# A recommendation tower on one core: a ring of two blocks of gathers in place of three, and transposes moved in the program of TensorE

## The reference, cut to what matters

```python
e = stack([tbl_f[ids[:, f]] for f in range(26)], axis=1)      # 512 x 26 x 128
sd = einsum('bfd,bd->bf', e, dense)                            # each embedding with the dense row
ss = einsum('bfd,bgd->bfg', e, e)                              # all pairs of embeddings
z = concatenate([dense, sd, ss[:, iu, ju]], axis=1)            # upper triangle: 325 pairs
h = concatenate([z, dense], axis=1)                            # 607 columns
h = maximum(h @ W_top1 + b_top1, 0)                            # 512
h = maximum(h @ W_top2 + b_top2, 0)                            # 256
y = h @ W_top3                                                 # 1
```

## Time and profile before

| what | value |
|---|---|
| median of 3 runs | 132.18 us (131.85 to 134.35) |
| the profiled execution | 132.72 us |
| its span in the trace | 130.9 us |
| PE busy | 94.0 us (72%) |
| DVE busy | 73.7 us (56%) |
| POOL busy | 67.5 us (52%) |
| ACT busy | 61.8 us (47%) |
| granted clock of TensorE, mean | 0.896 |

### The profile page before, as it was taken

The page is one execution under the profiler, slowest core; times in us unless marked ns, Lnnn a source line. Parts: engine busy times, 40 slices in busy tenths (PEclk is TensorE's granted clock), DMA queues, the critical chain, the costliest instruction groups (busy, mean ns, idle before and its releaser), DMA issues.

```text
span 130.9 us, 3331 instructions
## 1 busy us (share of the span) xinstructions
PE 94.0 (72%) x1420; PEld 78.2 (60%) x1420; DVE 73.7 (56%) x170; ACT 61.8 (47%) x131; POOL 67.5 (52%) x70
## 2 busy tenths in 40 slices
PE   0089899999969999000547459397784997897892
PEld 0157688888858887000436349286674796786780
DVE  1387999999997835000008927264370731974621
ACT  3435591966908506300308909164370904964410
POOL 2878888787888787770831725538172560000000
PEclk9999999999999999965557756999999559999999
DMA  2999965947996121220110110102011110000000
GB/s 53 242 379 367 272 242 185 267 115 179 381 372 207 44 60 40 63 59 21 44 41 8 45 40 25 49 16 60 25 38 43 25 40 25 0 5 0 8 0 1
DMA packets 6849, 13.37 MB, mean 102 GB/s; under 512 B 2353, under 2 KB 3506, under 8 KB 6834
## 3 DMA queue, kind: packets, MB, share of 16 engines
q1 hardware_dynamic: 4112, 8.95, 21.4%
q0 software_dynamic: 2048, 4.20, 11.2%
q10 hardware_dynamic: 674, 0.01, 0.3%
HBM read 13.15 MB, written 0.00 MB: 100 GB/s over the span
## 4 chain that ended last, share of the span: by engine, by line
PE 44%; POOL 17%; issue 15%; DMA 7%; another core or an unknown queue 6%; ACT 6%; DVE 2%; DVEq 0%; ACTq 0%
POOL rows L294 17%; PE gram L371 12%; PE hidden L398 8%; PE second L415 6%; PE gram L342 6%; DMA rows<-in_tables_gather,idx 5%; PE stage L325 5%; PE hidden L387 3%; PE hidden L342 2%; ACT Z L492 2%; ACT ET L470 2%; ACT ET L482 2%; PE second L413 2%; DVE Z L568 2%
## 5 line engine op out<-in xcount | busy, mean ns | idle before, releaser
L294 POOL DMA_INDIRECT rows<-in_tables_gather,idx x64 | 66.8, 1044 | 39.0 <-issue 17.4
L568 DVE COPY Z<-gram 32x112 f32<-32x112 f32 (+3 forms) x72 | 23.0, 320 | 35.5 <-PE gram L371 34.6
L371 PE MATMUL gram<-ET 128*32 128x27 f32 x1024 | 17.0, 207 | 25.8 <-issue 12.8
L492 ACT COPY Z<-gram 32x112 f32<-32x112 f32 (+1 forms) x72 | 23.2, 322 | 23.7 <-PE gram L371 22.9
L371 PEld LDWEIGHTS gram<-ET 128*32 128x32 f32 x1024 | 14.1, 123 | 29.4 <-issue 26.0
L552 DVE TENSOR_SCALAR onehot<-ids,rowid 128x1024 fp32r<-128x1024 int16 (+1 forms) x48 | 28.7, 659 | 5.1 <-DMA ids<-in_ids_one 2.1
L342 PE MATMUL gram<-onehot,part 128*128 128x512 f32 x80 | 22.5, 434 | 6.6 <-DVE part L558 6.2
L342 PEld LDWEIGHTS gram<-onehot,part 128*128 128x128 f32 x80 | 16.4, 211 | 10.7 <-DVE onehot L552 6.2
L342 PE MATMUL hidden<-onehot,part 128*128 128x512 f32 x80 | 19.7, 397 | 0.6 <-issue 0.6
L342 PEld LDWEIGHTS hidden<-onehot,part 128*128 128x128 f32 x80 | 14.6, 188 | 3.7 <-issue 0.8
L558 DVE TENSOR_TENSOR part<-raw,part 128x1024 fp32r<-128x1024 f32 (+2 forms) x11 | 12.1, 1123 | 3.1 <-issue 2.4
(11 more groups left out here) (38 smaller groups left out, 42.2 us busy)
## 6 DMA issues: line engine op xcount, KB each, us to landing
raw<-in_tables_one SPq DMA_DIRECT2D x9, 512.0 KB
ids<-in_ids_one SPq DMA_DIRECT2D x4, 256.0 KB, 5.5
rows<-in_tables_gather,idx POOLq DMA_INDIRECT x64
W1s<-in_W_pairs SPq DMA_DIRECT2D x1, 768.0 KB
W1d<-in_W_dense SPq DMA_DIRECT2D x1, 512.0 KB
W2s<-in_W_top SPq DMA_DIRECT2D x1, 512.0 KB
raw<-in_tables_one SPq DMA_DIRECT2D x1, 384.0 KB
ids<-in_ids_one SPq DMA_DIRECT2D x2, 128.0 KB, 3.6
```

The source lines that it names most:

```text
L294: pool.indirect_dma_start(out=rows[:, m % ROWS_RING, :], out_offset=None, in_=x["tables_gather"], in_offset=bass.IndirectOffsetOnAxis(ap=i ...
L371: last = pe.matmul(gram[p % 2][32 * i:32 * i + 32, NV * j:NV * (j + 1)], ET[:, VP * b:VP * (b + 1)], ETv[:, b, 0:NV], start=True, stop=True)
L492: last = act.copy(dst, src)
L568: last = dve.tensor_copy(dst, src)
```

## The change

The ring holds two blocks (8 gathers) where it held three (12). By L292 and L293, the gathers of block n now wait for the transposes of block n-2, not n-3, and block 2 is the first that waits, not block 3. The transposes of b4, b5 and b6 stand later among the look-ups: b4 after chunk 1 of group 4, b5 after its chunk 4, b6 after chunk 1 of group 5. The transposes of b8 to b12 stand one piece earlier, after pieces 0 to 4, and those of b13 stand after the Gram products of piece 5, ahead of its layers, where they stood behind the layers.

```diff
-ROWS_RING = 3 * GB
+ROWS_RING = 2 * GB
...
         AMID = {(0, 7): ["dense"], (1, 3): ["b0"], (2, 1): ["b1"], (2, 5): ["b2"], (3, 1): ["b3"],
-                (3, 6): ["b4"], (4, 3): ["b5"], (4, 7): ["b6"], (5, 7): ["b7"]}
-
-        SOON = {1: ["b8"], 2: ["b9"], 3: ["b10"], 4: ["b11"], 5: ["b12"]}
-        LATER = {5: ["b13"], 6: ["b14"], 7: ["b15"]}
+                (4, 1): ["b4"], (4, 4): ["b5"], (5, 1): ["b6"], (5, 7): ["b7"]}
+
+        SOON = {p: [f"b{p + 8}"] for p in range(6)}
+        LATER = {6: ["b14"], 7: ["b15"]}
```

## The result

The changed kernel takes 141.97 us (median of 4 runs, 141.34 to 142.56) beside 132.30 us for the kernel before: a ratio of 1.074 (95% interval 1.066 to 1.083). In a later comparison it was 1.077 (1.070 to 1.084). The prediction had the sign and the mechanism, but 137.4 us with a range up to 141.0; it was 4.6 us short. (Some executions of any of these kernels are slower at a lower granted clock; all ratios leave them out, and of e2 only one of four executions was free of this, so it has no ratio.) The profiled execution took 141.38 us, with a span of 139.5 us.

The account below looks back on a forecast made before the run. The prediction took a loop to bound the kernel: POOL's gathers stop PE, whose transposes release POOL. 132.72 + 0.75 (look-ups) + 4.50 (Gram stage) = 137.97, less 0.54, gave 137.4 us; range 132.0 to 141.0.

Parts of the forecast that it names:

- The loop: Gram stage: transposes release POOL, its four gathers stop PE, PE then finishes the piece and makes the next transposes; 7.69 us each.
- Six rounds: Gram stage: pieces 1 to 6 run beside the gathers of blocks 10 to 15; 46.14 us at 7.69 each.
- the five pairs of before: Earlier trace, blocks 10 to 14: PE comes free 0.97 to 1.04 us after each block's last gather.
- the look-up term: Look-ups: block 9's gathers end at 67.6, against 66.85 for block 10 before; +0.75 us (-3.65 to +1.85).
- products cost 0.235 us each: Look-ups: PE's price per product, from 16 products at 47.98 to 51.74, used for the 24 products of group 3.
- the end of the stop: Piece 0: PE is free 0.99 us after block 9's last gather; with the piece's rest, 2.09 us to b8's transposes.
- the late signal: End of the look-ups before: PE's signal reached ACT and POOL only after POOL's run of gathers; POOL restarted 3.00 us later.
- Gathers of block 3 in time: Rival, look-ups: block 3's gathers miss the weight loads and land in time, POOL stays at the low end; 133.0 us, chance 0.20.
- PE's stops not due to gathers: Rival: the stops are PE's own, say in its supply of small instructions, and signals come promptly; 127.6 us, chance 0.10.
- Late signals in the look-ups: Rival: chunks of groups 4 and 5 are signalled late while POOL runs, so b5 and b6 release it late; 140.4 us, chance 0.20.

Follow-up runs that it names:

- e2: Kernel before with the changed order of transposes but its ring of three blocks; 136.1 us against 133.0, from the one comparable execution.
- e11: Kernel before with blocks 10 to 15 loaded by SP as plain rows, not gathered by POOL (wrong rows); 117.0 us, ratio 0.866.
- e16: Kernel before with blocks 10 to 15 loaded by SP as plain rows, plus five POOL memsets at each of their releases; 116.2 us, ratio 0.867.
- e5: Kernel before with a ring of four blocks, on the chip where PE does not creep; 109.41 us against 109.35, ratio 1.010.
- e14: Changed kernel with SP loading the weights and masks only after b3's transposes; 139.0 us against 134.1 for the kernel before, ratio 1.038.
- e12: Kernel before, ring of three, with only the gathers of blocks 10 to 15 waiting for block n-2; 133.7 us against 132.7, ratio 1.008.
- e17: Kernel before with b13 to b15 ahead of the layers of pieces 5 to 7, blocks 10 to 14 waiting for block n-2; 133.3 us, ratio 0.998.
- e18: Kernel before with only b13, b14 and b15 moved ahead of the layers of pieces 5, 6 and 7, more rounds; 131.86 us against 132.96, ratio 0.991.
- e1: Kernel before with only the ring cut to two blocks, old order of transposes; 141.6 us against 133.0, ratio 1.059.
- e3: Changed kernel with b4, b5 and b6 back at their old places among the look-ups; 142.2 us, ratio 1.070 to the kernel before.
- e10: The changed kernel measured again, on a chip where PE creeps; 143.4 us against 132.7 for the kernel before.
- e4: Kernel before with only b13, b14 and b15 moved ahead of the layers of pieces 5, 6 and 7; first measurement, ratio 0.989.
- e15: Kernel before with a ring of four blocks, on a chip where PE creeps; 138.3 us against 134.1, ratio 1.034.

## Why the prediction was short

**The loop was right.** Six rounds were in the trace, each with PE free 0.85 to 0.94 us after the block's last gather (78.73 and 79.65 for block 10, 117.37 and 118.31 for block 15). From b8 to the end of piece 6 they took 46.57 us, where 46.14 had been forecast: 0.43 of the difference. e11 and e16 show that the cause is the right one, which the five pairs of before had only made likely. The rules cited from the Trainium skill (SBUF — State Buffer, Who interferes with whom), that a DMA never contends with a compute engine and that PE waits on nobody, don't hold for indirect transfers where PE creeps: the earlier trace rows and the 0.866 of e11 go against them. SP's plain loads in e11, and the gathers on e5's chip, agree with them.

**The step that failed is the look-up term**, "67.6 - 66.85 = +0.75 us". The path was right, its sizes weren't: it measured 69.14 - 66.85 = +2.29. Block 2's first gather took 3.05 us beside DVE's L558, not 1.97, so block 3's last one started at 31.12, not 30.2. It took 7.06 us to land, as taken from the earlier trace rows, so PE waited 6.03 us for it, not 5.0. Then "products cost 0.235 us each", a size read at full clock, failed: the transposes of b3 took 1.09 us, not 0.6, and the 24 products behind them 7.10 us, not 5.6. Three windows of the changed kernel show why; the first is of all engines, the other two of PE alone (busy us and count, granted clock, DMA share, GB/s):

```profile
30.00:40.00 10.00, 3.97 (x17) 3.13 (x16) 7.58 (x11) 5.26 (x7) 7.19 (x7) 0.76 0.96 310
```

```profile
41.00:42.00 1.00, 1.00 (x4) 0.50 0.28 66
42.00:43.00 1.00, 1.00 (x5) 0.99 0.25 61
```

After PE had been idle for 6.03 us its granted clock was 0.50 up to 42 us, and then 1.00. In the kernel before, PE was idle for no more than 1.03 us here, and the clock was 1.00 from 30 to 50 us; in e14, with a wait of 2.44 us, it stayed at 1.00 too. DVE was held up meanwhile, but the one-hots of those 24 products had been made by 33.98, before the wait was over, so it had no part in this. The wait was paid for again: some 3 us of products at half clock are 1.5 us lost, and the transposes lost 0.5. All this put the end of b4's transposes at 48.41, not 46.0, and block 6 started at 48.68, not 46.3.

The gathers of block 6 took 0.7 us more than taken. On the other side, b7's signal was not late: ACT took b7 at 61.51, and block 9 followed block 8 after 0.30 us, where a pause of 1.9 us had been forecast. Those 1.6 us hid part of the error above: +2.4, +0.7 and -1.6 make the 1.5 us by which the term was short. That they partly cancel is luck.

**The second size that failed is the end of the stop.** "0.99 us until PE is free" was read from single blocks of four gathers. After sixteen gathers without a pause it was 2.27 us (69.14 to 71.41); with the slower rest of piece 0, b8 came 3.49 us after the last gather, where 2.09 had been forecast: +1.40. A row that might have warned was there: in the earlier trace rows the late signal came 2.7 us after the end of a long run at 59.17. I read it as a delay of the look-ups' signal. It may have been the same stop: in the trace of e12, whose program is the same up to there, the signal was prompt, and piece 0 began at 53.84 and crept to 61.98 instead. That it is the same wasn't shown, and why the signal is late in some executions (the kernel before, e17) and prompt in others stays open.

**The sum.** 137.97 + 1.54 + 1.40 + 0.43 = 141.34, against 141.38 for the profiled execution. The other 1.1 us is the place of the profiled execution: 0.54 above the median before that the prediction had (132.18), 0.59 below the median after.

**The rivals.** Gathers of block 3 in time: no, 6.03 us. PE's stops not due to gathers (127.6 us): no, on chips like that of the case. Late signals in the look-ups (140.4 us, the nearest number): no, in the changed kernel they were prompt.

**What the parts cost.** The look-up waits alone 6.8%, 5.8 points of it from blocks 2 and 3; the Gram-stage waits alone 0.8%. Landing beside the weights makes half of the whole loss (7.4 to 3.8%). The order adds about 1.5 points to the ring's 5.9, with intervals that overlap; three late transposes moved earlier in the old kernel (e18) are a gain of 0.9%. The share of the order without the ring stays open (about 2%, from one execution).

## What to carry to other kernels

A smaller ring costs where the first wait falls, not where the steady state is: one pause of 4 us early in a serial chain of transfers moved block 3 into the stretch where the weights land, that stalled the consumer, its clock was at half for 4 us after the stall, and the stall came back as the next pause. A size read at full clock doesn't hold behind a stall. Price such a loop once around before calling a term small. Where one engine's transfers stop another, neither a larger nor a smaller ring helps by itself; what counts is which work stands beside the transfers.

A delay that was read after short runs of transfers needn't hold after a long one; here it doubled. And compare kernels on the same chip: here the two kinds of chip differ by more than any edit.

## What the runs showed of the hardware

- On most chips used, matrix products on small tiles (128x27) crept while POOL issued indirect transfers: after the first 29 to 60 records, 1 to 7 at a time, 0.7 to 2.1 us apart. They ran freely beside plain loads (129 records in 1.5 us with 91 GB/s landing, e11) and beside memsets (120 in 1.22 us, e16).
- The time from the last gather to PE's release was 0.8 to 1.1 us after blocks of four, where a piece was under way, and more after every longer run: 1.65 us after 8 gathers (e17), 1.9 to 2.6 after 16 (e1, e3, e10, e14, the changed kernel), 1.7 to 1.9 after 40 (e11, e12, e16), 2.4 to 2.7 after 44 (e2, e4, e18), 3.2 after 48 (e15). It doesn't simply grow with the length of the run; what sets it is open.
- On one chip there was no such stop, and the kernel before took 109.35 us in place of 132 to 134. What sets the chips apart is open.
- After a wait of 6.03 us the granted clock of PE was 0.50 (1.2 GHz) for the next 4 us and then 1.00; after one of 2.44 us (e14) it stayed at 1.00.
- One indirect transfer took 0.94 us of POOL alone, 1.97 beside a two-input DVE operation, and 3.05 where it began with a pair of those.
